# Edge attributes followed lane by lane, step by step, with the node update and the second norm between the steps

## The reference

```python
# layer 0
messages = relu(concat([x[row], x[col]]) @ W_msg + b_msg)
aggregated = segment_sum(messages, col)
h = relu(concat([x, aggregated]) @ W_upd + b_upd)
out = (h - mu) * rsqrt(var + LN_EPS) * gamma + beta
# layer 1
out1 = segment_sum(edge_attr, col)                  # 53125 x 96
cnt  = segment_sum(ones, col)
out2 = where(cnt > 0, segment_max(edge_attr, col), 0)
out3 = out1 / maximum(cnt, 1)
h = concat([x, out1, out2, out3, u[batch]])
h = relu(h @ W1 + b1) @ W2 + b2
```

## Time and profile before

| | us |
|---|---|
| median of three runs | 2734.12 (2732.61 to 2734.6) |
| the profiled execution | 2734.72 |
| its span in the trace | 2732.6 |
| opening, with the end of its stores | 0 to 126 |
| message pass | 126 to 674 |
| update and second norm | 674 to 751 |
| attribute pass | 751 to 1094 |
| node network | 1094 to 1470 |
| attention, third norm, pool table | 1470 to 2150 |
| best pass, to the end | 2150 to 2733 |

### The profile page before, as it was taken

One profiled execution on the slowest core, in us unless ns is written; L12 is line 12 of the kernel. 1 busy time (PEld: TensorE's weight loads), 2 busy tenths in 40 slices (PEclk: granted clock), 3 DMA queues, 4 the chain that ended last, 5 costly groups with the idle time before them and its releaser, 6 DMA issues. The chain is left out here.

```text
span 2732.6 us, 26946 instructions
## 1 busy us (share of the span) xinstructions
PE 1354.9 (50%) x7570; PEld 1070.0 (39%) x7570; DVE 1588.9 (58%) x3262; ACT 672.6 (25%) x1528; POOL 1390.0 (51%) x1444
## 2 busy tenths in 40 slices
PE   3577877877669999997993000000002411111104
PEld 2466766776569999554553000000001300000003
DVE  2467777776769999731213776677675334433432
ACT  1112222221547777111111000000002233333331
POOL 2177777776300000301104777777744377777774
PEclk9889999999879999998997555555555655555557
DMA  2477777875065564101002666666642466666664
GB/s 79 118 236 237 233 233 235 238 228 151 1 181 153 154 154 117 42 2 17 13 12 63 201 216 218 201 208 214 211 161 65 139 213 208 209 212 207 211 212 134
DMA packets 272030, 433.06 MB, mean 158 GB/s; under 512 B 108749, under 2 KB 181031, under 8 KB 271883
## 3 DMA queue, kind: packets, MB, share of 16 engines
q1 hardware_dynamic: 202635, 247.61, 27.3%
q0 software_dynamic: 66784, 183.09, 24.9%
q10 hardware_dynamic: 2464, 0.64, 0.1%
HBM read 302.15 MB, written 128.80 MB: 158 GB/s over the span
## 5 line engine op out<-in xcount | busy, mean ns | idle before, releaser
L1757 POOL DMA_INDIRECT att_rows<-att_table,lane_source x416 | 416.4, 1001 | 126.7 <-issue 126.7
L2083 POOL DMA_INDIRECT best_rows<-message_source_table,lane_source x416 | 393.3, 946 | 167.5 <-issue 126.4
L735 POOL DMA_INDIRECT msg_rows<-message_source_table,msg_index x416 | 400.0, 962 | 147.8 <-issue 125.2
L2194 DVE SCALAR_TENSOR_TENSOR best_state<-best_state,lane_line,best_ps_rows 128x256 f32<-128x256 f32 x416 | 199.8, 480 | 316.2 <-ACT best_ps_rows L2108 297.9
L863 PE MATMUL msg_ps_sum<-msg_by_edge,msg_rows 128*128 128x128 f32 x1664 | 232.4, 299 | 109.3 <-DVE aggT L795 107.6
L1789 PE MATMUL att_ps_upto<-ident,att_largest 128*4 128x128 f32 x1 | 0.4, 375 | 564.1 <-DVE att_largest L1854 564.1
L863 PEld LDWEIGHTS msg_ps_sum<-msg_by_edge,msg_rows 128*128 128x128 f32 x1664 | 218.0, 210 | 140.3 <-issue 139.1
L2108 ACT ACTIVATE best_ps_rows<-best_rows,lane_weight 128x256 f32<-128x256 f32 x416 | 173.5, 462 | 359.2 <-DMA best_rows<-message_source_table,lane_source 359.2
L2142 PE MATMUL best_ps_self<-w_selfT,hT 128*125 128x256 f32 x100 | 51.7, 671 | 398.3 <-DVE x L2200 387.2
L847 PE MATMUL msg_ps_window<-msg_window,msg_by_node 128*128 128x256 f32 x832 | 209.0, 397 | 26.5 <-DMA msg_window<-message_window_table 21.4
L1789 PEld LDWEIGHTS att_ps_upto<-ident,att_largest 128*4 128x4 f32 x1 | 0.1, 83 | 564.8 <-DVE att_largest L1854 564.8
(11 more groups left out here) (290 smaller groups left out, 2711.9 us busy)
## 6 DMA issues: line engine op xcount, KB each, us to landing
att_states<-aggT SPq DMA_DIRECT2D x104, 528.0 KB
msg_window<-message_window_table SPq DMA_DIRECT2D x416, 128.0 KB
best_states<-best_state SPq DMA_DIRECT2D x104, 512.0 KB
attr_rows<-in_edge_attr SPq DMA_DIRECT2D x103, 192.0 KB, 3.3
msg_line<-place_line SPq DMA_DIRECT2D x52, 256.0 KB, 4.9
attr_line<-mask_line SPq DMA_DIRECT2D x52, 256.0 KB, 3.9
attr_carry<-carry_line SPq DMA_DIRECT2D x52, 256.0 KB
msg_rows<-message_source_table,msg_index POOLq DMA_INDIRECT x416
```

Of the source, the lines that this page charges most:

```text
L735: nc.gpsimd.indirect_dma_start(rows[:, s, t, :], None, table, bass.IndirectOffsetOnAxis(ap=index[:, s, t:t + 1], axis=0)).then_inc(self.ro ...
L1757: nc.gpsimd.indirect_dma_start(rows[:, t % ring, :], None, self.attention_table, bass.IndirectOffsetOnAxis(ap=self.lane_source[:, t:t + 1] ...
L2083: nc.gpsimd.indirect_dma_start(rows[:, g % SLOTS, t, :], None, table, bass.IndirectOffsetOnAxis(ap=self.lane_source[:, g * TG + t:g * TG + ...
L2194: nc.vector.scalar_tensor_tensor(out=state[:, g % STATE_BUFS, t, :], in0=before, scalar=self.lane_line[:, n:n + 1], in1=weighed_row(n), op ...
```

## The change

Update, second norm and attribute pass become one block of code, `update_and_attributes`. Each of the 128 lanes is followed along its 416 edges: per step DVE runs one instruction for the maximum and one for the sum over 96 attributes. After every four steps comes a piece of the update, of the norm, or of a search for each node's last edge. The states (192 numbers per edge) go out to DRAM in 52 stores of eight steps, crossing runs are mended as in the best pass, and 25 indirect transfers fetch the state at each node's last edge, which PE turns into `aggT`. In the network the search and its round trip are gone. In the opening the lines `mask_line` and `carry_line`, `place_end` and 13 links of the chain are gone, the lists `before` and `after` too; the edge lists move from ACT's queue to POOL's, `base` to SP's, and SP stores the source table without waiting for the chain, with the one line left behind the fifth block. The update's weights are issued by ACT in the message pass, where SP issued them.

```diff
@@ opening
-        lines_made, lane_steps = 17, 16
+        lines_made, lane_steps = 4, 14
@@ SP
-                    sp.wait_ge(chain, lines_made)
-                    lines = ((self.mask_line, mask), (self.place_line, rel16), (self.carry_line, carry))
-                    for line, rows in lines:
-                        sp.dma_start(line.rearrange("(q r c) -> r q c", r=RT, c=P), rows[:]).then_inc(lines_out, 16)
+                    for tile, flat in first_nodes:
+                        sp.dma_start(tile, flat, allow_slow_non_contiguous=True).then_inc(lines_out, 16)
                     for b in range(NB):
+                        if b == edges_at:
+                            sp.wait_ge(chain, lines_made)
+                            sp.dma_start(self.place_line.rearrange("(q r c) -> r q c", r=RT, c=P), rel16[:]
+                                         ).then_inc(lines_out, 16)
                         sp.wait_ge(copied, b + 1)
...
@@ POOL, ACT
+                    pool.wait_ge(clears, 2)
+                    for tile, flat in transfers:
+                        pool.dma_start(tile, flat, allow_slow_non_contiguous=True).then_inc(loads, 16)
...
-                    act.wait_ge(clears, 4)
-                    for tile, flat in transfers:
-                        act.dma_start(tile, flat, allow_slow_non_contiguous=True).then_inc(loads, 16)
@@ sum_pass
-                    if ahead:
-                        self.load(sp, *ahead)
...
+                    if ahead:
+                        self.load(act, *ahead)
@@ update_and_attributes, SP
+                    for k in range(STEPS):
+                        sp.wait_ge(summed, (k + 1) * n)
+                        sp.dma_start(by_lane[:, k * n:(k + 1) * n, :], held[k % HELD]
+                                     ).then_inc(states_out[k % HELD], 16)
+                        if k + ROW_BUFS < STEPS:
+                            load(k + ROW_BUFS)
@@ update_and_attributes, DVE
+                    def step(t):
+                        k = t // n
+                        if t % n == 0:
+                            dve.wait_ge(*self.past(rows_in[k % ROW_BUFS], rows_upto(k)))
+                            if k >= HELD:
+                                dve.wait_ge(*self.past(states_out[k % HELD], 16 * (k // HELD)))
+                        row = row_bufs[k % ROW_BUFS][:, t % n, :]
+                        if t > 0:
+                            dve.wait_ge(maxed, t)
+                        nc.vector.scalar_tensor_tensor(
+                            out=maxima_of(t), in0=maxima_of(t - 1) if t > 0 else lowest[:],
+                            scalar=self.lane_line[:, t:t + 1], in1=row, op0=ALU.min, op1=ALU.max).then_inc(maxed, 1)
+                        if t > 0:
+                            dve.wait_ge(summed, t)
+                        nc.vector.scalar_tensor_tensor(
+                            out=sums_of(t), in0=sums_of(t - 1) if t > 0 else none[:, 0:AF],
+                            scalar=carry[:, t:t + 1], in1=row, op0=ALU.mult, op1=ALU.add).then_inc(summed, 1)
...
+                    for s in range(LANE // TG):
+                        for t in range(s * TG, (s + 1) * TG):
+                            step(t)
+                        chunk_work(s, update_work)
+                        search(s)
@@ mlp
-                    find_slices()
...
-                        if c == 1:
-                            find_edges()
@@ build
-            k.message_update(weights, *ahead)
-
-        k.normalize("norm1")
...
-            k.max_pass("attr", edgesT, ahead=ahead)
-            k.mlp(edgesT, weights, *ahead)
+            mlp_weights, mlp_ahead = k.mlp_weights(layer)
+            k.update_and_attributes(weights, *ahead, mlp_ahead)
+            k.mlp(k.aggT[0:AF + 1, 0:2, :], mlp_weights, *mlp_ahead)
```

More of the change, by code:

```diff
@@ L1109, in update_weights @@
         w = self.sb("upd_w", [P, 4, D], ctx=layer)
[L1110 to L1117 removed]
+        rows = {k: self.sb(f"upd_{k}", [1, D], ctx=layer) for k in ("b_upd", "beta")}
@@ new lines, in update_weights, with update_and_attributes @@
+        gamma = self.sb("upd_gamma", [NT, D], ctx=layer)
+        transfers = [(w[:], a["L0_gnn_W_upd"].rearrange("(k p) n -> p k n", p=P)),
+                     (gamma[:], self.row(a["L0_gnn_gamma"]))] + [
+            (tile[:], a[f"L0_gnn_{k}"].rearrange("(o d) -> o d", o=1)) for k, tile in rows.items()]
+        return (w, rows["b_upd"], gamma, rows["beta"]), (transfers, self.sem("upd_loads"))
+    def update_and_attributes(self, weights, transfers, loads, mlp_ahead):
+        nc, a = self.nc, self.a
@@ new lines, in update_and_attributes @@
+            at = [self.sb(f"search_at{k}", [P, NB], I32, ctx) for k in range(2)]
+            halves = (slice(0, NB // 2 + 1), slice(NB // 2 + 1, NB))
+            below = self.sb("search_below", [P, NB // 2 + 1, SPANS], BF16, ctx)
+            levels = self.sb("search_levels", [P, NB, SLICES], I32, ctx)
+            spans = levels[0:SPANS, :, :].rearrange("p b c -> p (b c)")
+            within = below[:].rearrange("p b c -> p (b c)")[:, 0:NB * SLICES].rearrange("p (b c) -> p b c", c=SLICES)
+            counts = self.sb("search_counts", [NT, NB], ctx=ctx)
@@ new lines, in turn, with spread_heads @@
+                    def turn(b):
+                        pe.wait_ge(made, n0 + b + 1)
+                        if b >= 2:
+                            pe.wait_ge(kept, n0 + b - 1)
+                        for k in range(2):
+                            last = nc.tensor.transpose(ps_turned[b % 2][:, k, 0:NT], self.h[:, b, k * P:(k + 1) * P],
+                                                       self.ident[0:NT, 0:NT])
+                        last.then_inc(turned, 1)
+                    def spread_heads():
+                        pe.wait_ge(heads_made, 3)
+                        nc.tensor.matmul(ps_heads[:, 0:SPANS], self.ones[0:SPANS, 0:P], diagonal, start=True, stop=True
+                                         ).then_inc(heads_spread, 1)
@@ new lines, in _ @@
+                    end = held[(STEPS - 1) % HELD][:, n - 1, :]
+                    pe.wait_ge(summed, LANE)
+                    for k in range(2):
+                        last = nc.tensor.transpose(ps_ends[:, k, :], end[:, k * AF:(k + 1) * AF], self.ident[:])
+                    last.then_inc(ended, 1)
+                    pe.wait_ge(scanned, 4)
+                    for k in range(2):
+                        last = nc.tensor.transpose(ps_heads[:, k * AF:(k + 1) * AF], ends[:, k, 0:P],
+                                                   self.ident[0:AF, 0:AF])
@@ new lines, in _ @@
+                    last.then_inc(back, 1)
+                    pe.wait_ge(relued, NB)
+                    pe.wait_ge(kept, n0 + NB)
+                    pe.wait_ge(fixed, 3)
+                    for b in range(NB):
+                        pe.wait_ge(*self.past(self.rows_in[b // fifth], 16 * fifth))
+                        if b >= len(ps_taken):
+                            pe.wait_ge(taken_kept[b % 2], (b - len(ps_taken)) // 2 + 1)
+                        ps = ps_taken[b % len(ps_taken)]
+                        for k in range(2):
+                            last = nc.tensor.transpose(ps[0:AF + 1, k, 0:NT], neigh[0:NT, b, k * AF:(k + 1) * AF + 1],
+                                                       self.ident[0:NT, 0:NT])
+                        last.then_inc(taken, 1)
@@ new lines, in _ @@
+                    nc.vector.scalar_tensor_tensor(
+                        out=whole[:, AF:2 * AF], in0=ps_heads[:, AF:2 * AF], scalar=carry[:, 0:1],
+                        in1=first[:, AF:2 * AF], op0=ALU.mult, op1=ALU.add).then_inc(fixed, 1)
+                    dve.wait_ge(searched, found_all + 2)
+                    for k in range(HELD):
+                        dve.wait_ge(*self.past(states_out[k], 16 * len(range(k, STEPS, HELD))))
+                    nc.vector.tensor_copy(neigh[0:NT, :, 2 * AF:2 * AF + 1], counts[:].unsqueeze(2)).then_inc(fixed, 1)
@@ L1225, in mlp_weights @@
+        for k in range(5):
+            self.before[self.rows_in[k].name] += 16 * fifth
+        self.spare += [(s, NB) for s in (multiplied, based, relued, stats, centred, added, taken)]
+        self.spare += [(s, LANE) for s in (maxed, summed)]
     def mlp_weights(self, layer):
```

806 lines of the change are left out of this document (385 added, 421 removed).

## The result

The changed kernel takes **2552.8 us** (median of four runs, 2549.7 to 2556.0) against 2733.4 for the kernel before: a ratio of 0.934, 95% interval 0.932 to 0.936. That is 181 us less. The prediction was 2561, with a range from 2525 to 2625. The profiled execution took 2549.7, with a span of 2548.0.

The account below looks back on a forecast made before the run. PE (373) and DVE (369) were both busy in the 420 us of update, norm and attributes; waits bounded the opening and stalled the network. 37 + 118 + 19 = 174 off 2734.7 gave 2561 us, range 2525 to 2625.

Parts of the forecast that it names:

- Opening, 37: Opening: earlier first kept block 25.2, faster 25 blocks 2, shorter end, and SP's lists 1.7 sooner; together 37 us off.
- The lower bound of the opening, 12: Opening: only its end moves, 12 us off for 37, if POOL's edge lists land late; as a rival 2586 us, 8%.
- Distance of a step, 0.235: New block: DVE's step instructions start 0.235 us apart at 96 columns; 832 of them take 195.5 us.
- DVE's list, 250: New block: DVE's steps plus the pieces between them take 250 us, and the block lasts as long as this list.
- What hides the rest: New block: PE's and ACT's update and norm work, 77 us in the old blocks, is covered by DVE's 250.
- Transfers, nothing: New block: moving 61 MB takes 157 to 235 us of the transfer engines, below 250, so it costs nothing.
- Network, 19: Node network: 14.9 stall, 2.6 half clock behind it and 1.8 slice heads go, 0.5 charged; 19 us off.
- The 1.8 for the slice heads: Start of the network, where PE has no cover: spreading the slice heads goes, 1.8 us off.
- The number costs nothing: Rival, steps: the per-partition number adds nothing at this width, 0.175 per instruction, 50 us less, 2511; 8%.
- every instruction waits out the one ahead: Rival, steps: each instruction waits for the one before, 0.37 each, 112 us more, 2673; 9%.
- The transfers did not hold DVE: Rival, new block: transfers or lists hold DVE, some 40 of the 235 us show, 2601; 10%.
- The slower rival: Rival, steps: distance does not shrink with width, as the per-partition number is read after the pipe empties; 254 more, 2815; 3%.

Follow-up runs that it names:

- b_stores: Kernel before, with SP storing the 25 source-table blocks as they are copied and the three chain lines only after the 18th block: ratio 0.998 to the kernel before.
- a_serial: Changed kernel, with all pieces of update, norm and search ahead of the first step instead of between the steps: 2932.6 us, 0.973 of the kernel before.
- a_late_more: Changed kernel, with POOL clearing an idle tile 97 times before its first scatter in the network, once the ring is full: 2843.2 us, 0.944 of the kernel before.
- a_narrow24: Changed kernel, with each step instruction over 24 of the 96 attributes, rows and stores still moved in full: 2819.9 us, 0.937 of the kernel before.
- a_chain: Changed kernel, with each step instruction made to wait for the one just ahead: 2946.7 us, 0.976 of the kernel before.
- a_late: Changed kernel, with POOL clearing an idle tile 28 times before its first scatter in the network, once the ring is full: 2811.1 us, 0.933 of the kernel before.

## Why the prediction was right, point by point

- **Opening, 37: measured 40** with the message pass. The mechanism was right, the three terms were off both ways. The first kept block is at 22.41 and not 20.8 (the second part of `x` landed at 19.55, where I took 17.9). The run of 25 blocks is 58.6, so it loses 8.0, and not the 2 that I gave to "13 links and four turns, mostly under PE"; of the 8, the runs show 3 for the backlog of stores and 2.3 for the links and turns; the rest lies between the first trace and the later ones and stays open. The end comes 7.4 behind the last bias, where I took 5. That the sum is off by 2 alone (-1.6, +6.0, -2.4) is in part luck.
- **The lower bound of the opening, 12 "if nothing but SP's order helps"**: b_stores shows 10 at the opening's end, and 6 in the kernel's time.
- **Distance of a step, 0.235: measured 0.228.** It was built from three parts, and each has been taken apart since: 0.060 for the number per partition (0.060 assumed), 1.03 ns a column, and no wait for the instruction before the last. 832 x 0.228 = 190 for 195.5.
- **DVE's list, 250: measured 244.5** with 3.9 of waits in it; so the pieces between the steps took 50.5 where I had 54.5. Start 4.6 for 4.5, and tail 48.7 for 48: both as forecast.
- **"What hides the rest"** held, but the margin was not what I said. PE was busy not for 77 us but for 141 of the 249 (134 in a_serial), and each row of 25 gathers of the search took POOL some 49 us and not 31 ("gathers at 1.25" is true of the tail alone). Both were still covered.
- **Transfers, nothing: right.** 0.81 of 249 us, inside the 157 to 235 that I had from two rates, and 190 us of steps ran over them without a wait in a_serial.
- **Network, 19: measured 20.9.** 14.9 for the stall, shown by a_late_more to be all lost time, and 2.2 behind it (1.6 in a_late_more). The 1.8 for the slice heads was mis-sized: the first product comes 0.3 sooner after the start, and 1.9 are gained in all before the stall. The last 2.0 lie behind the last product, and were not forecast. Half clock at the new start cost nothing to speak of: mean clock 0.62 in the first 15.8 us, 0.68 in the same stretch before, and then 1.00.
- **The rivals.** "The number costs nothing" and "every instruction waits out the one ahead" both fell by the trace, and the experiments say what each would have been worth in the steps: 42 off and 120 on, where I had 50 and 112. The transfers did not hold DVE. The opening moved at both ends. The slower rival needed a distance that does not shrink with the width; it is 0.41 at 260 columns, 0.228 at 96 and 0.154 at 24.
- Not forecast: 1.7 off in attention, which I leave open.

## What to carry to other kernels

Two serial chains on one vector engine, issued in turn, cost per instruction the distance between independent ones and not the instruction's length: here 0.23 us for 0.35. The work of other engines fitted under this stream of 244 us, which had 3.9 of waits at its start and no gap behind them, even though by itself it would take 179; only DVE's own share of it, 50 us, was paid. Ask first whether each engine's own sum stays below the stream. In a_narrow24 that was not enough: every sum stayed below, and the stream still lost 43 us while POOL issued its gathers. And when a block ends in a row of gathers, look at how many of them the next block's first piece needs: the rest can be issued inside it.

## What the runs showed of the hardware that I had not expected

- **POOL's gathers and the engines beside them.** Beside DVE's full stream of 96 columns a gather of POOL takes 1.3 to 1.9 us (median, by run and row of gathers) and up to 4.2, for 0.94 otherwise, and DVE's stream keeps without a gap. In a_chain, a_narrow24 and a_serial POOL keeps 0.94, and other engines start up to 17.9 us behind the end of what they wait for. The Trainium skill's page "SBUF — State Buffer", section "🔬 SBUF: two separate sides", says that DVE and POOL share a port pair which whoever starts first holds for the whole instruction (for a DVE instruction with two inputs in this memory, only against a POOL instruction that reads it), and that PE and ACT never wait on anyone. The changed kernel's trace agrees in that POOL pays beside a full stream of such instructions. The late signals are not covered by this rule: in a_narrow24 it was ACT that stood for 17.8 us, with PE's product ended, and DVE waited behind it. What delayed them stays open.
- **A ring's slack is time, not rows.** Four rows covered 16 us of lateness without a trace in the total (a_late); with 55 us (a_late_more) ACT waited 22 for its fifth row.
- **The same kernel took 10% longer in the later runs** (3014 and 3016 us on two chips for 2733), nearly all of it in passes that gather (665 us for 546 in the message pass), while the middle and the network agree within 0.3%. Whether the chip or something else made the difference stays open. The ratio of the two kernels moved by less than its interval.
